# The hand-over from the MLP to the cross-attention: last norm applied on ScalarE, tiles and first query heads in another order, first mean squares folded in two parts

## What is computed

```python
x = _layernorm(x + _L0_attn_ref(x, ...))     # mamba2, then h + silu(h2 @ gate.T) * (h2 @ up.T) @ down.T
x = _layernorm(x + _L0_xattn_ref(x, ctx_4096, mask, Wq, Wk, Wv, Wo, q_norm_w, k_norm_w))
x = _layernorm(x + _L0_ffn_ref(x, router_w, A, B))

def _layernorm(x, axis=-1, eps=1e-05):
    m = jnp.mean(x, axis=axis, keepdims=True)
    v = jnp.var(x, axis=axis, keepdims=True)
    return (x - m) / jnp.sqrt(v + eps)

# in _L0_xattn_ref
q = _rmsnorm(q, q_norm_w); k = _rmsnorm(k, k_norm_w)      # over the 128 elements of a head
scores = jnp.einsum('bhqd,bhkd->bhqk', q, k) * scale + mask
out = jnp.einsum('bhqk,bhkd->bhqd', softmax(scores), v) @ Wo.T
```

## Time and profile before

| | us |
|---|---|
| median of 3 runs (lowest, highest) | 1035.24 (1034.44, 1035.61) |
| the profiled execution | 1037.25 |
| its span on the core | 1035.4 |
| busy: TensorE / its weight loads | 981.2 / 810.1 |
| busy: VectorE / ScalarE / GpSimd | 601.9 / 483.9 / 409.1 |
| chain of work that ended last | PE 85%, VectorE 9%, ScalarE 2%, GpSimd 1% |

### The profile page before, as it was taken

One profiled execution on the slowest core, in us unless ns is written; L12 is line 12 of the kernel. 1 busy time (PEld: TensorE's weight loads), 2 busy tenths in 40 slices (PEclk: granted clock), 3 DMA queues, 4 the chain that ended last, 5 costly groups with the idle time before them and its releaser, 6 DMA issues.

```text
span 1035.4 us, 15422 instructions
## 1 busy us (share of the span) xinstructions
PE 981.2 (95%) x5008; PEld 810.1 (78%) x5008; DVE 601.9 (58%) x1357; ACT 483.9 (47%) x1361; POOL 409.1 (40%) x338
## 2 busy tenths in 40 slices
PE   5897999999999998799999999999999999999795
PEld 3664687788888886688888888888888888888672
DVE  4879555222212256566666666766566666666776
ACT  4644444121322244555554654654655655555433
POOL 4435737333424351353342442432623524523311
PEclk9999999999999999899999999999999999999997
DMA  6110114101111111011011010020020110100002
GB/s 211 42 41 0 42 44 162 61 0 61 61 61 61 41 61 55 20 42 41 21 41 41 20 56 25 20 81 0 20 81 0 53 49 0 61 0 0 1 1 82
DMA packets 12975, 45.58 MB, mean 44 GB/s; under 512 B 1616, under 2 KB 2256, under 8 KB 9872
## 3 DMA queue, kind: packets, MB, share of 16 engines
q1 hardware_dynamic: 12944, 45.20, 12.4%
HBM read 43.10 MB, written 2.10 MB: 44 GB/s over the span
## 4 chain that ended last, share of the span: by engine, by line
PE 85%; DVE 9%; issue 2%; ACT 2%; DMA 2%; POOL 1%; SPq 0%; DVEq 0%; ACTq 0%
PE bank L354 24%; PE bank L355 24%; PE bank L356 24%; PE bank L624 5%; PE bank L634 3%; DVE cbuf L1539 2%; DMA raw_b<-in_ctx_t 1%; DVE xbc L1555 1%; PE bank L364 1%; PE bank L708 1%; PE bank L611 1%; DMA res<-in_x 1%; DVE ctx_lo L1484 1%; DVE bst L1714 0%; PE bank L737 0%
## 5 line engine op out<-in xcount | busy, mean ns | idle before, releaser
L354 PE MATMUL bank<-act_hi,w_hi 128*128 128x512 f32 x560 | 228.4, 408 | 6.3 <-DVE act_lo L1484 3.9
L356 PE MATMUL bank<-act_hi,w_lo 128*128 128x512 f32 x560 | 222.6, 398 | 0.0
L355 PE MATMUL bank<-act_lo,w_hi 128*128 128x512 f32 x560 | 222.5, 397 | 0.0
L1421 POOL TENSOR_TENSOR pb<-pb,prec 128x512 f32<-128x512 f32 x64 | 66.6, 1040 | 315.2 <-DVE prec L1840 315.2
L1124 ACT ACTIVATE pb<-pb,nmax 128x128 f32<-128x128 f32 x256 | 99.7, 391 | 83.8 <-DVE nmax L1835 83.8
L354 PEld LDWEIGHTS bank<-act_hi,w_hi 128*128 128x128 f32 x560 | 107.7, 192 | 31.9 <-issue 7.3
L355 PEld LDWEIGHTS bank<-act_lo,w_hi 128*128 128x128 f32 x560 | 107.5, 192 | 24.1 <-issue 2.2
L356 PEld LDWEIGHTS bank<-act_hi,w_lo 128*128 128x128 f32 x560 | 107.3, 192 | 23.4
L354 PE MATMUL bank<-w_hi,ot_hi 128*128 128x512 f32 x256 | 107.0, 418 | 2.9 <-DVE ot_lo L1484 2.9
L355 PE MATMUL bank<-w_lo,ot_hi 128*128 128x512 f32 x256 | 101.0, 395 | 0.0
L356 PE MATMUL bank<-w_hi,ot_lo 128*128 128x512 f32 x256 | 100.5, 392 | 0.0
(11 more groups left out here) (179 smaller groups left out, 2093.9 us busy)
## 6 DMA issues: line engine op xcount, KB each, us to landing
raw_a<-in_w_q SPq DMA_DIRECT2D x8, 1024.0 KB, 4.7
raw_b<-in_w_o SPq DMA_DIRECT2D x8, 1024.0 KB, 4.8
raw_a<-in_w_gu SPq DMA_DIRECT2D x7, 1024.0 KB, 5.3
raw_b<-in_w_kv SPq DMA_DIRECT2D x8, 512.0 KB, 3.2
raw_b<-in_w_dn SPq DMA_DIRECT2D x7, 512.0 KB, 3.4
res<-in_x SPq DMA_DIRECT2D x8, 256.0 KB, 6.0
raw_b<-in_ctx_t SPq DMA_DIRECT2D x8, 256.0 KB, 3.7
xre<-in_x SPq DMA_DIRECT2D x2, 1024.0 KB, 7.2
```

The source lines that it names most:

```text
L354: mm(o, l_hi, r_hi, start=first, stop=False)
L355: mm(o, l_hi, r_lo, start=False, stop=False)
L356: return mm(o, l_lo, r_hi, start=False, stop=last)
L1421: TT(pb[:, jj % 2, :, :], pb[:, jj % 2, :, :], prec[:, jj % 2, :].unsqueeze(2).to_broadcast([P, GH, L]), ALU.mult).then_inc(p_norm, 1)
```

## The change

The layer norm of tiles 16 to 23 is applied by ScalarE to `res` itself, `rstd * x + bias`, with a bias of -mean * rstd that VectorE makes (`ln_bias`); `xn` and the copy back go out of use there, and PE turns `res`. Tile 20 is turned in the last MLP step and tiles 21 to 23 after the first three query heads, so all four ahead of the fourth. VectorE's low part of tile 20 moves out of the MLP step, behind the last sum and its statistics, and GpSimd's root for the keys moves behind that of tile 23. The mean squares of heads 0 to 2 of the first half are folded, summed with eps and raised to the power apart from head 3; the fold of the three stands on PE ahead of the next query head, that of the fourth behind it. In the first slot VectorE takes `v_rest` ahead of `q_part(0, 1, 0)` and the reciprocal of the sums, and GpSimd does three splits of output weights, not two, ahead of the first scale of the probabilities.

```diff
@@ TensorE
                 for k in range(KT):
-                    t = nc.tensor.transpose(banks[i % 2][:, k * P:(k + 1) * P],
-                                            xn[:, i % 2, k * P:(k + 1) * P], ident)
+                    ks = slice(k * P, (k + 1) * P)
+                    t = nc.tensor.transpose(banks[i % 2][:, ks], xn[:, i % 2, ks] if i < 16 else res[:, i - 16, ks],
+                                            ident)
...
                             kv_step(0, 0, b - 3)
+                        else:
+                            pe.wait_ge(h_done, 4 * MLP_IT)
+                            norm_t(20, (bank[4], bank[5]))
...
             pe.wait_ge(n_lo, 20)
-            pe.wait_ge(h_done, 4 * MLP_IT)
             for h in range(GH):
                 q_step(0, 0, h)
-                norm_t(20 + h, (bank[4], bank[5]))
+                if h < 3:
+                    norm_t(21 + h, (bank[4], bank[5]))
             kt_step(0, 0)
+            pe.wait_ge(ld_small[7], 16)
+            pe.wait_ge(o_add, 8 + 8 * MLP_IT)
+            pe.wait_ge(qp_done, 3)
+            mm(bank[7][:, 0:48], fold[:, :], qpart[:, 0, 0:48], start=True, stop=True).then_inc(qsa_mm, 1)
             pe.wait_ge(n_lo, 24)
             q_step(0, 1, 0)
-            pe.wait_ge(o_add, 8 + 8 * MLP_IT)
-            pe.wait_ge(ld_small[7], 16)
-            qs_step(0, 0)
+            pe.wait_ge(qp_done, 4)
+            mm(bank[7][:, 48:64], fold[:, :], qpart[:, 0, 48:64], start=True, stop=True).then_inc(qs_mm, 1)
             s_step(0, 0)
@@ ScalarE
-            def res_copy(i):
-
-                act.wait_ge(n_x, i + 1)
-                A(res[:, i - 16, :], xn[:, i % 2, :], ACT.Copy).then_inc(res_x, 1)
-
+            def ln_apply(i):
+
+                act.wait_ge(n_b, i - 15)
+                A(res[:, i - 16, :], res[:, i - 16, :], ACT.Identity, bias=lnb[:, i - 16:i - 15],
+                  scale=rstd[:, i:i + 1]).then_inc(n_x, 1)
+
+            ln_apply(16)
             for i in range(16, 20):
-                res_copy(i)
                 norm_hi(i, tb)
+                ln_apply(i + 1)
                 kv_evac(0, 0, i - 16)
...
             for h in range(GH):
-                res_copy(20 + h)
+                norm_hi(20 + h, (bank[4], bank[5]))
+                if h < 3:
+                    ln_apply(21 + h)
                 q_evac(0, 0, h)
-                norm_hi(20 + h, (bank[4], bank[5]))
@@ GpSimd
-                if i == 22:
-                    k_rsqrt(0, 0)
-            q_rsqrt(0, 0)
+            k_rsqrt(0, 0)
+            q_rsqrt_part(qva_done, 0, 3, qra_done)
+            q_rsqrt_part(qv_done, 3, 4, qr_done)
             wo_rest(0, 0)
             wo_rest(0, 1)
+            wo_rest(0, 2)
             p_scale(0, 0)
-            wo_rest(0, 2)
             wo_rest(0, 3)
@@ VectorE
-            def ln_x(i):
-
-                b = i % 8
+            def ln_bias(i):
+
                 dve.wait_ge(n_rstd, i + 1)
-                dve.wait_ge(n_t, i - 1)
-                TS(xn[:, i % 2, :], res[:, b, :], mv[:, i, 0:1], rstd[:, i:i + 1], ALU.subtract, ALU.mult)\
-                    .then_inc(n_x, 1)
+                STT(lnb[:, i - 16:i - 15], mv[:, i, 0:1], -1.0, rstd[:, i:i + 1], ALU.mult, ALU.mult)\
+                    .then_inc(n_b, 1)
...
                         if b >= 1:
-                            ln_x(15 + b)
+                            ln_bias(15 + b)
...
-                        if b >= 2:
-                            norm_lo(14 + b, tb if b < 6 else (bank[4], bank[5]))
+                        if 2 <= b < 6:
+                            norm_lo(14 + b, tb)
...
                 if j == 0:
                     v_rest(pg, pn, 0)
+                if not before:
+                    q_part(0, 1, 0)
+                    softmax_rec(0, 0)
...
+            norm_lo(20, (bank[4], bank[5]))
+            ln_bias(23)
             k_var(0, 0)
-            ln_x(23)
+            norm_lo(21, (bank[4], bank[5]))
             q_part(0, 0, 0)
+            k_norm(0, 0)
             norm_lo(22, (bank[4], bank[5]))
-            k_norm(0, 0)
             q_part(0, 0, 1)
             norm_lo(23, (bank[4], bank[5]))
             q_part(0, 0, 2)
+            q_var_part(qsa_mm, 0, 3, qva_done)
             q_part(0, 0, 3)
-            q_var(0, 0)
-            dve.wait_ge(res_x, 8)
+            q_var_part(qs_mm, 3, 4, qv_done)
+            dve.wait_ge(n_x, 24)
             dve.wait_ge(ld_small[4], 16)
+            dve.wait_ge(qra_done, 1)
             softmax_max(0, 0)
-            q_part(0, 1, 0)
-            softmax_rec(0, 0)
             slot(0, 0, before=False)
```

More of the change, by code:

```diff
@@ L68, in build_program @@
         rstd = sb(ctx, "rstd", [P, 48])
+        lnb = sb(ctx, "lnb", [P, B])
         bst = sb(ctx, "bst", [P, 2, 6])
@@ L171, in build_program @@
         n_t, n_hi, n_lo, n_bn, n_mv = sem("n_t"), sem("n_hi"), sem("n_lo"), sem("n_bn"), sem("n_mv")
-        res_x, vlo_done = sem("res_x"), sem("vlo_done")
+        n_b, vlo_done = sem("n_b"), sem("vlo_done")
+        qsa_mm, qva_done, qra_done = sem("qsa_mm"), sem("qva_done"), sem("qra_done")
         x_add = sem("x_add")
@@ L1410, in q_rsqrt, with q_rsqrt_part @@
                     .then_inc(qr_done, 1)
+            def q_rsqrt_part(ready, h0, h1, done):
+                pool.wait_ge(ready, 1)
+                TT(qr[:, h0:h1, :].rearrange("p h j -> p (h j)"), qv[:, h0:h1, :].rearrange("p h j -> p (h j)"),
+                   pow_m[:, 0:(h1 - h0) * HALF], ALU.pow).then_inc(done, 1)
             def k_rsqrt(g, n):
@@ L1820, in q_var, with q_var_part @@
                 t.then_inc(qv_done, 1)
+            def q_var_part(ready, h0, h1, done):
+                dve.wait_ge(ready, 1)
+                for tb in range(4):
+                    rows_ = slice(32 * tb, 32 * tb + 32)
+                    t = TS(qv[rows_, h0:h1, :].rearrange("p h j -> p (h j)"),
+                           bank[7][rows_, h0 * 16:h1 * 16].rearrange("p (c t) -> p c t", t=4)[:, :, tb],
+                           HD * EPS, None, ALU.add)
+                t.then_inc(done, 1)
             def softmax_max(g, jj):
```

## The result

| | before | after |
|---|---|---|
| median, us (lowest, highest; runs) | 1035.42 (1034.44, 1037.49; 6) | 1025.73 (1023.79, 1029.49; 6) |
| ratio after / before, 95% interval | | 0.9901 (0.9884 to 0.9919) |
| the profiled execution / its span | 1037.25 / 1035.4 | 1024.56 / 1022.7 |

The slices of the page, TensorE alone, stand beside the earlier trace rows; the dent is still there, one slice of 8 tenths.

The account below looks back on a forecast made before the run. TensorE was taken to bound the kernel except in the dent between MLP and cross-attention. The steps through the first slot gained 7.0 us, with no difference from the clock: 1035.24 - 7.0 = 1028.2 us, range 1025.8 to 1031.5.

Parts of the forecast that it names:

- What bounds the kernel, and the dent: TensorE bounds nearly everything from the MLP on; other engines' work counts only in the dent, the MLP's hand-over to cross-attention.
- Apply on ScalarE: Layer norm of tiles 16 to 23: ScalarE hides the extra 1.4 us except at tile 16, costing TensorE 0.45 us.
- Tile and head order, first fold: Between fourth and next query head: waits mostly go, next head runs at full clock, ending at 410.05, 5.5 us sooner.
- Mean squares in two parts: Query norm of the first half: 12-column power hidden under the next query head, only the fourth head's 1.02 us on the path.
- VectorE takes the V split first: First slot: V split reached at 416.7, ahead of 1.3 us of transpose and reduce, which delays the reciprocal.
- Table load: ScalarE before the exponentials: 1.28 us load, sum stays at 7.0; rival that exponentials are held behind it gives 1029.7, chance 0.15.
- To the end of the slot: First slot: K/V step starts at 417.2, TensorE goes on at 422.5 instead of 429.64; gain taken as 7.0 us.
- The clock behind it: Two gaps of about 2 us stay; one clock fall as before, no difference; bounds 1.8 us gain or loss.
- the rival of no fall: Hand-over: the two gaps, shorter together, bring no clock fall, gaining 1.8 us more: 1026.4 us, chance 0.15.
- two falls: Hand-over: both remaining gaps bring the clock down, a loss of 1.8 us: 1030.0 us, chance 0.08.
- the four cases that it takes in: Whole kernel: forecast 1028.2, no clock fall 1026.4, exponentials held behind the table load 1029.7, two falls 1030.0 us.
- Queues: SP's loads and GpSimd's splits move with the last apply; TensorE is full from there, so nothing takes the gain back.

Follow-up runs that it names:

- a_nopad: Kernel after with its biases in unused columns of `rstd` instead of the new tile, so all tiles lie as before: 1030.94 us, ratio 0.9937 to the kernel before.
- u_t20: Kernel after with tiles 20 to 23 turned behind the first four query heads: 1030.51 us, hand-over (add of tile 17 to first output add) 60.1 us.
- u_split: Kernel after with mean squares of all four heads folded and raised to the power at once, behind the next query head: 1029.26 us in one execution.
- u_order: Kernel after with the next head's transpose, reduce and the reciprocal of the sums back ahead of the V split in the first slot: 1025.02 us.
- a_align: Kernel after with 32 unused bytes ahead of `cbuf`, shifting the Mamba-2 tiles alone: 1025.89 us, ratio 0.9892 to the kernel before.
- a_sh32: Kernel after with 32 more unused bytes a partition behind the biases' tile: 1031.22 us in one execution.
- a_sh64: Kernel after with 64 more unused bytes a partition behind the biases' tile: 1026.11 us in one execution.
- b_pad: Kernel before with the new tile `lnb` allocated but unused, so later tiles lie 32 bytes further on: 1031.9 us, ratio 0.9950.

## Why the prediction was right, and where it fell short

- *What bounds the kernel, and the dent.* Right. All that the order gained stands in that one place (a_nopad), and what was found elsewhere is not of the order.
- *Apply on ScalarE.* Cost forecast 0.45 us, measured 0.44 at tile 16; the apply took 0.81 us a tile, as the earlier trace rows said. ScalarE worked 16.67 of the 27.5 us for the 13.9 forecast, since the stretch now holds other work too, and nothing of it reached TensorE.
- *Tile and head order, first fold.* Right: waits of 0.18 and 0.26 us, and the head at clock 1.00. That the turns are what it rests on, u_t20 shows.
- *Mean squares in two parts.* Right: 12 columns took 2.27 us under the query head, then 4 took 1.01. The step counted no gain for the power itself; by u_split the direct one is 1.42 us of the 7.0, and 2.9 with the clock.
- *VectorE takes the V split first.* Harmless, and without effect (u_order).
- *Table load.* Right to leave the sum as it was. The load runs from 411.81 for 1.28 us and the first exponential starts at 413.10, with no idle time between. The Trainium skill ("ScalarE: Activation LUTs", What ACT_TABLE_LOAD costs) puts a drain of 1.38 us on top; in this trace there is none, behind the load or ahead of it (the splits end at 411.79).
- *To the end of the slot.* K/V step 0.3 us later than forecast, the product with V 0.2.
- *The clock behind it.* One fall, as forecast, in two of three profiled executions of the kernel after (hand-over 56.18 and 56.09). The third had none (54.59), and the kernels a_align, a_sh32 and a_sh64, which have the same instructions with tiles elsewhere, had two (57.6 to 57.8). So the rival of no fall is not another outcome of the kernel but another execution of it; that two falls are too is likely and was not seen with its own placement. Each fall moves the hand-over by 1.5 us, near the 1.8 that was the bound.
- *The range.* Its upper end does not follow from its terms: the slowest of the four cases that it takes in is 1030.0, and 0.6 us for the small bounds make 1030.6, not 1031.5. The lower end, 1026.4 less 0.6, does, and the time fell below it.
- *The step that failed* is the one that the sum does not have. "Queues" said of the stretch behind the hand-over that TensorE is full there, "so nothing takes the gain back", and the sum let all stages but one stand as they were. The new tile was costed as operations on it and never as an allocation ahead of the operands of every matmul. It was worth 0.26 us in each of the MLP's steps and 0.72 in each group; b_pad puts it at 5.2 us with nothing else changed. The step that the sum does have came out near its size: a_nopad, the order without the tile, gained 6.5 us for the 7.0 forecast. The 5.2 and the 7.0 make more than the 9.7 measured, most likely because the forecast was taken from a median about 2 us low: from 1037.3, less 7.0 and 5.2, come 1025.1.

No row of the trace of before shows what another placement would give. But that its matmuls of 512 columns followed each other at 237.5 ns with `h_hi` and at 226.7 with `act_hi`, at the same clock and with nothing waited for, could be read there, and it says that something beside the number of columns sets the pace.

## What to carry to other kernels

Where a change adds, removes or resizes an on-chip tile, treat it as an edit to every later tile: compare the spacing of untouched matmuls before and after, and run the allocation alone and the edit without it, before the gain is put down to the code. Where one engine bounds all but one dent, measure the dent from a mark that both kernels share, in more than one execution; then each part of the order can be priced alone, and parts that do nothing, or cost, show. A wait is worth its own length plus what the clock does behind it, and that second part may differ from one execution to the next.

## What the hardware showed that was not expected

- Matmuls of 512 columns at full clock, their instructions unchanged, followed each other at 226 to 237.5 ns depending on where tiles begin in a partition. For `w_lo` with `h_hi` and with `y_hi` it was least when the two lay a multiple of 256 bytes apart, and moving `w_lo` by 128 bytes changed it in both directions (232.1 to 226.2, 227.8 to 230.6). The reason stays open, and other pairs do not follow that rule.
- The kernel after had no clock fall in the hand-over in one execution and one in two others; the same instructions with tiles elsewhere had two. Each was worth 1.5 us.
- GpSimd's power by columns: 1.01 us for 4, 2.27 for 12, 2.91 for 16.
